# Feed-forward stage of a decoder kernel: order of the normalising, the SiLU, the magnitude and the value product around the second tile's rounding

## The reference

```python
def bit_linear(x, w, b):
    gamma_x = clip(max(abs(x), axis=-1), 1e-05)
    scale_x = 127.0 / gamma_x
    x_dq = clip(round(x * scale_x), -128, 127) / scale_x
    w_dq = clip(round(w / gamma_w), -1, 1) * gamma_w      # gamma_w = mean(abs(w))
    return x_dq @ w_dq.T + b
gate = silu(bit_linear(x, gate_w, gate_b))                # 256 -> 1024
val = bit_linear(x, val_w, val_b)                         # 256 -> 1024
out = bit_linear(gate * val, out_w, out_b)                # 1024 -> 256
x = x + out                                               # x inside is layernorm(x)
...
```

## Time and profile before

| what | value |
|---|---|
| median of three executions | 1179.49 us |
| lowest, highest | 1173.73, 1180.12 us |
| the profiled execution's own time | 1175.87 us |
| its span, first to last instruction | 1174.1 us |
| mean granted clock of TensorE in it | 0.951 of 2.4 GHz |
| busy in the span: TensorE, VectorE, ScalarE, GpSimd | 88%, 72%, 57%, 27% |
| feed-forward stage in the span | about 84 to 187 us |

### The profile page before, as it was taken

The page is one execution under the profiler, slowest core; times in us unless marked ns, Lnnn a source line. Parts: engine busy times, 40 slices in busy tenths (PEclk is TensorE's granted clock), DMA queues, the critical chain, the costliest instruction groups (busy, mean ns, idle before and its releaser), DMA issues.

```text
span 1174.1 us, 21695 instructions
## 1 busy us (share of the span) xinstructions
PE 1032.6 (88%) x6383; PEld 719.0 (61%) x6383; DVE 850.6 (72%) x2422; ACT 669.1 (57%) x2046; POOL 319.8 (27%) x528
## 2 busy tenths in 40 slices
PE   7887886899989957899999999999999999967495
PEld 5664544666666634566767657667576666745384
DVE  5677764777887767877778878787788786744285
ACT  2687783655555625667555585575655755631262
POOL 3333322222112322313222222222232222202366
PEclk8899997999999978999999999999999999989598
DMA  9700001221111003200000000000000000001731
GB/s 274 269 22 16 1 1 45 64 55 55 54 54 54 19 1 93 66 4 13 1 14 1 1 15 1 15 1 1 16 1 1 14 1 14 1 1 50 239 108 38
DMA packets 38876, 49.59 MB, mean 42 GB/s; under 512 B 5107, under 2 KB 29563, under 8 KB 38528
## 3 DMA queue, kind: packets, MB, share of 16 engines
q1 hardware_dynamic: 36160, 44.16, 12.6%
q0 software_dynamic: 2304, 4.24, 1.0%
q10 hardware_dynamic: 320, 0.15, 0.1%
HBM read 32.70 MB, written 14.78 MB: 40 GB/s over the span
## 4 chain that ended last, share of the span: by engine, by line
PE 40%; issue 6%; ACT 5%; POOL 4%; DVE 2%; SPq 1%; DMA 0%; DVEq 0%; POOLq 0%; ACTq 0%
PE PS L1854 33%; PE PS L2251 3%; POOL out_dram L1415 3%; PE PS L2231 3%; ACT arena L1705 2%; ACT arena L1713 1%; POOL small L1323 1%; PE PS L2253 1%; PE PS L2108 1%; SPq L1189 1%; DVE small L878 0%; ACT mask L1689 0%; ACT EW L1645 0%; ACT EW L1640 0%; DVE X L870 0%
## 5 line engine op out<-in xcount | busy, mean ns | idle before, releaser
L1854 PE MATMUL PS<-early,arena 128*32 128x256 f32 (+6 forms) x928 | 118.2, 353 | 45.5 <-DVE early L712 23.7
L1328 POOL TENSOR_SCALAR small<-small 128x4 f32<-128x4 f32 x64 | 17.8, 279 | 421.1 <-ACT mask L1689 248.7
L1854 PE MATMUL PS<-EW,arena 128*128 128x256 f32 (+7 forms) x512 | 115.6, 349 | 11.3 <-DVE small L846 8.4
L1854 PE MATMUL PS<-wq,EW 128*128 128x512 f32 x256 | 123.2, 604 | 1.5 <-DVE arena L822 1.5
L1854 PE MATMUL PS<-wo,early 128*128 128x256 f32 x512 | 116.1, 386 | 7.1 <-DVE sinT L897 6.4
L1705 ACT ACTIVATE arena<-arena,small 128x128 f32<-128x128 f32 (+3 forms) x256 | 119.5, 475 | 4.1 <-DVE small L851 4.1
L1854 PEld LDWEIGHTS PS<-early,arena 128*32 128x32 f32 (+4 forms) x928 | 59.6, 118 | 98.0 <-issue 34.5
L1854 PEld LDWEIGHTS PS<-wo,early 128*128 128x128 f32 x512 | 99.1, 194 | 27.7 <-issue 7.8
L1854 PEld LDWEIGHTS PS<-EW,arena 128*128 128x128 f32 x512 | 84.7, 193 | 40.4 <-issue 33.2
L846 DVE CUSTOM_DVE_ANT_0 arena<-PS,kmask 128x128 f32<-128x128 f32 (+3 forms) x256 | 91.0, 388 | 21.2 <-PE PS L1854 16.4
L1689 ACT ACTIVATE mask<-PS 128x128 f32<-128x128 f32 x256 | 67.1, 281 | 47.6 <-PE PS L1854 47.3
(11 more groups left out here) (340 smaller groups left out, 2404.1 us busy)
## 6 DMA issues: line engine op xcount, KB each, us to landing
EW<-in_masksT_dram SPq DMA_DIRECT2D x32, 256.0 KB, 3.5
tokens_dram<-EW SPq DMA_DIRECT2D x1, 4160.0 KB, 15.1
arena<-tokens_dram SPq DMA_DIRECT2D x16, 260.0 KB, 3.4
results_dram<-EW SPq DMA_DIRECT2D x32, 128.0 KB, 3.2
EW<-results_dram SPq DMA_DIRECT2D x4, 1024.0 KB
X<-in_x_dram SPq DMA_DIRECT2D x8, 256.0 KB, 4.6
wq<-in_wq_dram SPq DMA_DIRECT2D x1, 2048.0 KB, 10.5
wo<-in_wo_dram SPq DMA_DIRECT2D x1, 2048.0 KB, 18.0
```

Of the source, the lines that this page charges most:

```text
L1854: return pe.matmul(dst, lhs, rhs, start=first, stop=last)
```

## The change

It exchanges steps within the second tile of a batch on three engines. No instruction is added or taken away.

- VectorE: `prepare(b + 2)` (the rows' magnitude) stands ahead of `narrow(b, 0)` (the add), for batches 0 to 5.
- ScalarE: `applied(b + 2)` (normalising, batches 0 to 5) and `gated(b + 1, 0)` (the next SiLU, batches 0 to 6) stand ahead of `quantised(b, 1)` (the rounding), and in that order.
- TensorE: `value(b + 1, 0)` stands ahead of `down(b, 0)`, for batches 0 to 6.

```diff
@@ VectorE, def ffn(b, par, left)
                     if type(b) is int and b == 0 and j == 0:
                         read_out(B - 1)
+                    if j == 1 and left == 2:
+                        prepare(b + 2, par)
                     if j == 1:
                         narrow(b, 0)
                     elif type(b) is not int or b > 0:
...
                         ln_stats(SELF, 0)
-                    if j == 1 and left == 2:
-                        prepare(b + 2, par)
@@ ScalarE, def ffn(b, par, left)
                     if j == 0:
                         gated(b, 1, par)
+                    if j == 1 and left == 2:
+                        applied(b + 2)
+                    if j == 1 and left > 0:
+                        gated(b + 1, 0, 1 - par)
                     quantised(b, j)
                     if j == 0 and left > 0:
                         levels(b + 1)
-                    if j == 1 and left > 0:
-                        gated(b + 1, 0, 1 - par)
-                    if j == 1 and left == 2:
-                        applied(b + 2)
@@ TensorE, def ffn(b, par, left)
                     elif left > 0:
                         gate(b + 1, 0)
+                    if j == 1 and left > 0:
+                        value(b + 1, 0)
                     if j == 1:
                         down(b, 0)
...
                     if j == 0:
                         value(b, 1)
-                    elif left > 0:
-                        value(b + 1, 0)
```

## The result

The changed kernel took 1164.11 us, the median of four runs (1161.37 to 1168.77), against 1177.81 us for the kernel before (four runs, 1173.73 to 1180.12): a ratio of 0.9891 with a 95% interval of 0.9844 to 0.9939. It is faster, as forecast, but by more: 13.7 us by the medians where 6.7 had been forecast, and the range ended at 1165.5. The profiled execution took 1165.95 us, its span is 1164.1 us.

A forecast was written before the change was run, and what follows sets the result against it. A ring of waits through several engines was taken to bound the feed-forward's batches. 85.64 - 78.0 - 0.93 (late start) gave 6.7 us gain, so 1172.8 us against 1179.49, range 1165.5 to 1178.5.

The forecast's parts named there:

- The old ring: Feed-forward batch before: VectorE's magnitude waits for ScalarE's normalising, which stands behind the rounding only by program order; 12.25 us.
- The new ring: Feed-forward batch after: ScalarE's own order, two rounding-to-eviction legs of 2.48 us and six steps of 1.00; 10.96 us.
- The cost of VectorE's and TensorE's moves: Feed-forward: later add on VectorE and later `down` on TensorE were to cost nothing, except in batch 6.
- The 0.5 us charged to TensorE's move in batch 6: Batch 6 has no normalising or magnitude to hide the move, so its rounding was to come 0.5 us later.
- one-time work: VectorE's work behind batch 1, 2.42 us before; about 1.2 us was to stay, making batch 1 to 2 12.2 us.
- 78.0: Forecast sum in us of the feed-forward's seven lengths between second-tile roundings, against 85.64 before.
- The clock: TensorE behind the one-time work: full clock with a gap of about 1 us; a fall would cost up to 2 us.
- A: Feed-forward: ScalarE's ring bounds, gain 5 to 8.5 us; the forecast itself, chance 0.58.
- B: Feed-forward: TensorE closes the ring, half a microsecond more per batch, gain about 3 us, 1176.5; chance 0.20.
- C: Clock falls behind the one-time work as before, or in a new place: gain 4.5 to 5 us, 1175; chance 0.10.
- D: Slower: normalising at the head of ScalarE's queue waits for GpSimd's scales, 0.9 us spare; 1187 us, chance 0.05.
- E: No effect: a hidden wait at the start of self attention takes the gain back, 1179 us; chance 0.07.

The follow-up runs named there:

- the two unrolled kernels: Kernel before and changed kernel, each with feed-forward batches 2 to 5 written out instead of looped: 1168.09 and 1169.14 us, one execution each, beside 1178.33 for the kernel before.
- The repeat: The changed kernel measured again with nothing edited: 1167.95 us, eight runs, against 1178.33 for the kernel before, ratio 0.9924.

## Why the prediction was right in kind and wrong in size

*The old ring.* Right. Normalising alone ahead of the rounding removes it; the SiLU alone removes a part. The other two edits alone leave VectorE waiting, 3.29 us in one piece. VectorE's waits for the normalising are under 1 us each, as forecast.

*The new ring.* Right: ScalarE's order, with 2.48 us from rounding to eviction and steps of 1.00. The sum gave 10.96 us; it measures 10.88 to 10.96. ScalarE idles 1.18 us ahead of the eviction, for the rounding that now stands last. The Trainium skill ("TensorE: Matmul & The Clock Gate", the section on architectural detail) has ScalarE and VectorE as strictly in-order queues. The trace agrees: the level rounding stood ready behind the waiting eviction and did not pass it, and moved ahead by program order it filled most of the gap.

*The cost of VectorE's and TensorE's moves.* Right at nothing for batches 0 to 5: all seven lengths make 74.89 with them and 74.92 without. The 0.5 us charged to TensorE's move in batch 6 was wrong; that batch takes 9.26 us with and without it, and with the SiLU's move alone.

*The failing step: "In the loop the old ring lasted 12.25 and 12.82 against 11.95 in straight line, so I add 0.3 to each, and 0.4 where the loop turns".* The loop's cost was carried from the ring that was removed to the one that replaced it. It belonged to VectorE's leg, as the two unrolled kernels show, and came to nothing in the new ring: 10.88, 10.96 and 10.88 us looped, 10.94, 10.94 and 10.95 written out. That is 34.3 forecast against 32.72 measured, 1.6 us. With "10.7" for batch 5 to 6 (10.10: one step less than the ring's 10.96, plus some tenths of slack that weren't there) and "9.8" for batch 6 to 7 (9.26) another 1.1 us went, and 0.1 and 0.3 in the first two (of the 2.42 us of one-time work 0.93 stayed, where 1.2 had been forecast). In all 78.0 was 74.89: the gain of the stage is 9.8 us, not 6.7.

*The range.* Its low end was a gain of 14.0 us against 1179.49. The ring gives 9.8. The rest of the way to 1164.11 is no term of the sum; it is, as far as these runs show, chance in the medians of three and four executions that lie 6 to 7 us apart: the kernel before read 1175.37 with 19 runs and 1178.33 with 13, the changed kernel 1164.11 with four and 1167.95 with eight. The repeat is inside the range, the first measurement 1.4 us below it. I had put the spread on the low side too narrowly.

*The clock.* It came as forecast: behind the one-time work the changed kernel stays at 1.00 (second length 1.00 against 0.84 in the earlier trace rows), with TensorE's gap under 1 us instead of 2.96. That the shorter gap is the reason is not shown. With the normalising alone ahead the gaps there are 0.89 and 0.93 us, and the clock fell behind them: eight transposes took 1.92 us instead of 1.06. With the level rounding early they are 1.28 and 0.93 us, and it stayed. First the former, then the latter:

```profile
111.89 1.36 PE L1854 MATMUL PS<-early,arena 128*128 128x512 bf16 x6 [0.89 <-DVE arena L629]
...
115.24 1.92 PE L2036 MATMUL PS<-ident,arena 128*128 128x128 f32 x8
```

```profile
112.56 1.36 PE L1854 MATMUL PS<-early,arena 128*128 128x512 bf16 x6 [1.28 <-DVE arena L629]
...
115.68 1.06 PE L2036 MATMUL PS<-ident,arena 128*128 128x128 f32 x8
```

The Trainium skill's rule on the clock gate (the same page, its part on the gate), that an idle TensorE falls back to half rate and sustained work releases it, does not tell these two apart. Bounding its price by 2 us was too much for this place: moving the work away altogether gave 2.71, 2.42 of it the work itself.

*The rivals.* A: the ring is ScalarE's, but the gain of the stage, 9.8 us, lies above its 5 to 8.5. B was refuted for the change, but the order with the level rounding early shows how near it was: one more step out of ScalarE's ring and a ring through TensorE closes at 10.55. C: no fall behind the one-time work, but one ahead of the stage, 1.24 us. The repeat shows it too (9.71 us from product to rounding, at a clock of 0.82), and so does the SiLU alone; ScalarE's part alone doesn't (8.58 us). Nothing edited has run by then, so it is not an effect of the change. D exists and has 0.74 us of room in an ordinary batch, near the 0.9 given. E: in the profiled pair self attention's first maximum comes 10.3 us earlier and the end 10.0, so the later stages took the shift all but whole.

## What to carry to other kernels

When an edit cuts a ring of waits, walk the new ring with legs from the trace and take over no surcharge of the old one: ask of loop overhead, one-time work and short clock falls on which engine's leg they lay, and whether that leg is in the new ring. In an in-order queue, put ahead of a late-fed step only what the old ring waits for, and leave behind it what can fill the gap that its own consumer opens: here the normalising ahead and the SiLU behind beats both ahead, 9.95 to 10.40 us against 10.88 to 10.96 in an ordinary batch. Measure such a change between two equal events inside the loop; here that repeated to 0.01 us between two profiles of the changed kernel, while whole executions of one kernel lay 6 to 12 us apart.

## What the runs showed of the hardware

The hardware loop of two passes cost the kernel before 1.25 us in three batches, on VectorE's leg, and the changed kernel, where VectorE waits in each batch, nothing. The stage's lengths repeat within 0.01 us between two profiles of one program, but its start doesn't: its first product came at 82.85 to 92.05 us in these profiles, without any edit ahead of it. The sixteen matmuls that start just ahead of it took 3.71 us in ten of the thirteen profiles (granted clock 1.00 where read) and 5.25 or 5.26 in three, at 0.67 or 0.68, with no edit ahead of them. A fall of the clock behind the one-time work went with gaps of 2.96 us and of 0.89 and 0.93 us, and gaps of 1.28 and 0.93 us went without one. A VectorE instruction on two elements a partition took 1.24 us instead of 0.17, beside a GpSimd addition that ended with it.
